# Side-by-side runs in the first layer, a_lo products one step behind, and x, weights and biases on other queues, in a four-layer graph network on one core

## The reference, cut to what matters

```python
h = jnp.maximum(_layernorm(x, axis=-1), 0.0)
x = x + L0(h)      # A_row @ h @ W_in + A_col @ h @ W_out, A and A.T each divided by its row sums
h = jnp.maximum(_layernorm(x, axis=-1), 0.0)
x = x + L1(h)      # two passes: swish(adj @ h @ W + b), then again on the result
h = jnp.maximum(_layernorm(x, axis=-1), 0.0)
x = x + L2(h)      # relu(D A_hat D @ h @ W + b), A_hat = adj + I, D from its row sums
h = jnp.maximum(_layernorm(x, axis=-1), 0.0)
x = x + L3(h)      # relu(D A_hat D @ (h @ W) + b)
```

## Time and profile before

| | before |
|---|---|
| median of three runs | 1110.06 us |
| the profiled execution, its own time | 1109.7 us |
| its span in the profile | 1107.9 us |
| TensorE matmuls busy | 1093.9 us (99%) |
| VectorE busy | 1044.1 us (94%) |
| ScalarE busy | 921.6 us (83%) |
| GpSimd busy | 31.4 us (3%) |
| mean rate from and to HBM | 368 GB/s |
| granted TensorE clock, mean | 1.00 of full speed |

### The profile page before, as it was taken

How to read it: one execution, slowest core, us unless ns; L and a number is a source line. 1 busy time by engine, 2 the same in 40 slices (tenths; PEclk the granted TensorE clock), 3 DMA queues, 4 the chain that set the end, 5 groups by cost and what they waited for, 6 DMA issues and landing times.

```text
span 1107.9 us, 14636 instructions
## 1 busy us (share of the span) xinstructions
PE 1093.9 (99%) x4992; PEld 909.1 (82%) x4992; DVE 1044.1 (94%) x1427; ACT 921.6 (83%) x1313; POOL 31.4 (3%) x30
## 2 busy tenths in 40 slices
PE   6999999999999999999999999999999999999998
PEld 5888888888888888888888888888888887888886
DVE  7899998999999999989989899999989999999997
ACT  7999997799788688888787788888888888887774
POOL 2000000000000000000000011121100000000000
PEclk9999999999999999999999999999999999999999
DMA  9999999999998999999999999999999999999992
GB/s 349 409 409 406 403 404 352 367 390 409 369 370 314 345 409 409 409 399 363 340 376 402 382 344 362 355 364 367 359 393 349 380 348 359 381 366 405 356 359 112
DMA packets 113835, 408.35 MB, mean 369 GB/s; under 512 B 12641, under 2 KB 13921, under 8 KB 113761
## 3 DMA queue, kind: packets, MB, share of 16 engines
q1 hardware_dynamic: 113760, 407.42, 96.6%
HBM read 405.27 MB, written 2.10 MB: 368 GB/s over the span
## 4 chain that ended last, share of the span: by engine, by line
PE 85%; DVE 13%; issue 1%; DMA 1%; ACT 0%; SPq 0%; ACTq 0%
PE bank L806 54%; PE bank L810 27%; DVE a_lo L553 10%; PE bank L827 3%; DVE stats L611 1%; DMA raw<-in_adj_t_dram 1%; DVE x_sb L705 0%; DVE zt L696 0%; DVE raw L547 0%; DVE h_lo L604 0%; PE bank L817 0%; DVE mv L615 0%; DVE acc L547 0%; PE bank L819 0%; DVE lnscale L627 0%
## 5 line engine op out<-in xcount | busy, mean ns | idle before, releaser
L553 DVE TENSOR_TENSOR a_lo<-raw,a_hi 128x1024 fp32r<-128x1024 f32 x560 | 657.5, 1219 | 31.1 <-ACT a_hi L410 14.0
L806 PE MATMUL bank<-a_hi,h_hi 128*128 128x512 f32 x1400 | 436.7, 393 | 8.8 <-ACT a_hi L412 8.8
L410 ACT ACTIVATE a_hi<-raw 128x1024 fp32r<-128x1024 f32 x368 | 378.7, 1056 | 68.4 <-PE bank L810 57.7
L810 PE MATMUL bank<-a_lo,h_hi 128*128 128x512 f32 x1400 | 433.1, 391 | 0.9 <-DVE a_lo L553 0.8
L806 PE MATMUL bank<-a_hi,h_lo 128*128 128x512 f32 x1400 | 432.1, 390 | 0.0
L810 PEld LDWEIGHTS bank<-a_lo,h_hi 128*128 128x128 f32 x1400 | 262.5, 188 | 58.9 <-DVE a_lo L553 4.6
L806 PEld LDWEIGHTS bank<-a_hi,h_hi 128*128 128x128 f32 x1400 | 260.3, 189 | 60.1 <-issue 8.7
L806 PEld LDWEIGHTS bank<-a_hi,h_lo 128*128 128x128 f32 x1400 | 263.6, 188 | 55.3
L412 ACT ACTIVATE a_hi<-raw 128x1024 fp32r<-128x1024 f32 x192 | 201.9, 1054 | 24.5 <-PE bank L810 10.6
L553 DVE TENSOR_TENSOR a_lo<-acc,a_hi 128x1024 fp32r<-128x1024 f32 x144 | 170.7, 1217 | 6.3 <-ACT a_hi L410 4.6
L410 ACT ACTIVATE a_hi<-acc 128x1024 fp32r<-128x1024 f32 x144 | 147.6, 1060 | 23.9 <-PE bank L810 22.6
(11 more groups left out here) (79 smaller groups left out, 403.3 us busy)
## 6 DMA issues: line engine op xcount, KB each, us to landing
raw<-in_adj_t_dram SPq DMA_DIRECT2D x496, 512.0 KB, 7.0
acc<-in_adj_t_dram SPq DMA_DIRECT2D x144, 512.0 KB, 6.3
raw<-in_adj_dram SPq DMA_DIRECT2D x128, 512.0 KB, 8.0
out_dram<-x_sb SPq DMA_DIRECT2D x7, 256.0 KB, 4.6
x_sb<-in_x_dram SPq DMA_DIRECT2D x3, 512.0 KB, 9.1
x_sb<-in_x_dram SPq DMA_DIRECT2D x2, 256.0 KB, 3.1
out_dram<-x_sb SPq DMA_DIRECT2D x2, 128.0 KB, 1.7
w_sb<-in_L_gnn_W_dram SPq DMA_DIRECT2D x3, 64.0 KB, 9.0
```

The lines of the kernel that those rows point to most:

```text
L410: act.activation(sub_hi_of(n), sub_raw(n), ACT.Copy).then_inc(sub_hi, 1)
L553: dve.tensor_tensor(sub_lo_of(n), sub_raw(n), sub_hi_of(n).bitcast(F32), ALU.subtract).then_inc(sub_lo, 1)
L806: pe.matmul(bank[half][:, :], weights, hi_a[:, half * GW:(half + 1) * GW], start=start and weights is hi_w, stop=False)
L810: last = pe.matmul(bank[half][:, :], hi_w, lo_a[:, half * GW:(half + 1) * GW], start=False, stop=stop)
```

## The change

It does five things.

- **Order.** The three first runs go side by side: block 0 with d = 1, 2, 3, then block 1, and so on, steps 0 to 23. That makes blocks 2 and 3 of h due at step 6, 4 and 5 at step 12, 6 and 7 at step 18. The next run (number 3) takes the fourth pair of banks, and all later ones move to another pair (`run_banks`, `run_prior`, `pair_of`).
- **a_lo behind.** From step 4 on TensorE does the a_lo pair of a step behind the a_hi matmuls of the next one (`LO_BEHIND`). ScalarE's place is free once the a_hi matmuls of its former step are done (`hi_used`) and VectorE has read it; VectorE now waits for `sub_used` itself, with each a_lo.
- **The first layer norm.** Blocks 0 and 1 stay with VectorE. Blocks 2 to 7 go the way of the later ones, in pairs: bias by VectorE, Relu and h_hi by ScalarE, h_lo by VectorE, at the steps in the tables. GpSimd does none.
- **Queues.** ScalarE asks for x blocks 0 and 1 at its start, 2 and 3 behind its step 0, 4 to 7 behind its step 3. GpSimd asks for the rest of x, the weights and the biases, each behind a step of VectorE. SyncE has tiles alone.
- **Drains.** The copies of the first three runs stand behind steps 25 to 30.

```diff
+        for i in range(CB):
+            for d in range(1, NG):
+                seq.append((d - 1, 0, d, i, i == 0, i == CB - 1))
+                if i == CB - 1:
+                    runs.append((0, d, 0))
+                    run_end.append(len(seq) - 1)
         for b in range(NG):
-            for kind in range(2):
+            for kind in range(1 if b == 0 else 0, 2):
...
+        def run_banks(r):
+            return z_ps if r == 3 else run_ps[r % 3 if r < 3 else (r - 1) % 3]
+
+        def run_prior(r):
+            return None if r <= 3 else r - 4 if r <= 6 else r - 3
...
-        DRAIN = {run_end[r] + 7 - 3 * (runs[r][2] >= 2) + half: (r, half) for r in range(len(runs)) for half in range(2)}
+        DRAIN = {run_end[r] + (4 + r if r < 3 else 7, 7, 4, 4)[runs[r][2]] + half: (r, half)
+                 for r in range(len(runs)) for half in range(2)}
...
-        FIRST_STATS = {24: 4, 36: 5, 50: 6, 64: 7, 77: 8, 90: 9}
+        FIRST_STATS = {2: 1, 6: 2, 11: 3, 24: 4, 36: 5, 50: 6, 64: 7, 77: 8, 90: 9}
-        FIRST_AFFINE = {29: 4, 41: 5, 55: 6, 69: 7, 82: 8, 95: 9}
-        FIRST_RELU = {32: 4, 44: 5, 58: 6, 71: 7, 84: 8, 97: 9}
+        FIRST_AFFINE = {3: 1, 8: 2, 13: 3, 29: 4, 41: 5, 55: 6, 69: 7, 82: 8, 95: 9}
+        FIRST_RELU = {4: 1, 9: 2, 14: 3, 32: 4, 44: 5, 58: 6, 71: 7, 84: 8, 97: 9}
...
-        LOAD_X = {16: 2, 36: 3, 62: 4}
-        LOAD_W = {72 + 3 * i: i for i in range(5)}
-        LOAD_B = {87 + 3 * i: i for i in range(3)}
+        X_BLOCKS = [FIRST[0], FIRST[1], (GB, CB)] + [(b, b + CB) for b in range(CB, NB, CB)]
+        LOAD_X_ACT = {0: 1, 3: 2}
+        LOAD_X = {8: 3, 28: 4, 54: 5}
+        LOAD_W = {62 + 3 * i: i for i in range(5)}
+        LOAD_B = {77 + 3 * i: i for i in range(3)}
...
@@ gpsimd
+            for n in range(S0):
+                if n in LOAD_X or n in LOAD_W or n in LOAD_B:
+                    pool.wait_ge(sub_lo, n + 1)
+                if n in LOAD_X:
+                    i = LOAD_X[n]
+                    blocks = slice(*X_BLOCKS[i])
+                    pool.dma_start(x_sb[:, blocks, :], x[:, blocks, :]).then_inc(x_in[i], 16)
...
@@ scalar
                 if sub_before[n] is not None:
-                    act.wait_ge(sub_used, sub_before[n] + 1)
+                    act.wait_ge(sub_lo, sub_before[n] + 1)
+                    act.wait_ge(hi_used, sub_before[n] + 1)
...
@@ vector
                 dve.wait_ge(sub_hi, n + 1)
+                if sub_before[n] is not None:
+                    dve.wait_ge(sub_used, sub_before[n] + 1)
...
@@ tensor
+            def products(n):
+                hi_products(n)
+                if n > LO_BEHIND:
+                    lo_products(n - 1)
+                if n < LO_BEHIND:
+                    lo_products(n)
```

More of the change, by code:

```diff
@@ L35, in build_gnn_stack @@
     S0 = 2 * NG * NB
+    LO_BEHIND = 3
     ctx = ExitStack()
@@ L82, in build_gnn_stack @@
         std0, rstd0, bias0 = (zt[:, 384 + i * NB:384 + (i + 1) * NB] for i in range(3))
-        x_in = [sem(f"x_in{i}") for i in range(NG + 1)]
+        x_in = [sem(f"x_in{i}") for i in range(NG + 2)]
         const_in = sem("const_in")
@@ L374, in _ @@
                                base=0, pattern=[[-1, P]], channel_multiplier=1).then_inc(ident_made, 1)
[L376 to L387, removed]
+            weights = (w_in, w_out, w1, w2, w3)
+            biases = (b1, b2, b3)
+            for n in range(S0):
[5 more added lines that the diff above has]
+                    pool.dma_start(x_sb[:, blocks, :], x[:, blocks, :]).then_inc(x_in[i], 16)
+                if n in LOAD_W:
+                    i = LOAD_W[n]
+                    pool.dma_start(w_sb[:, i, :], weights[i]).then_inc(const_in, 16)
+                if n in LOAD_B:
+                    i = LOAD_B[n]
+                    pool.dma_start(b_sb[:, i, :], biases[i].rearrange("(a n) -> a n", a=1).to_broadcast([P, D]))\
+                        .then_inc(const_in, 16)
             for q in range(NQ):
@@ L799, in _, with operands, hi_products @@
         def _(pe):
-            def products(n, hi_w, lo_w, bank, start, stop):
-                hi_a, lo_a = sub_hi_of(n), sub_lo_of(n)
+            def operands(n):
+                if n < S0:
+                    r, _, _, k, first, last = seq[n]
+                    return h_hi[0][:, k, :], h_lo[0][:, k, :], run_banks(r), first, last
+                sweep, g, k = passes[n - S0]
+                src = SET_OF[sweep - 1]
+                return h_hi[src][:, k, :], h_lo[src][:, k, :], banks_of(sweep, g), k == 0, k == NB - 1
+            def hi_products(n):
+                hi_w, lo_w, bank, start, _ = operands(n)
                 pe.wait_ge(sub_hi, n + 1)
@@ L805, in products, with lo_products @@
                     for half in range(2):
-                        pe.matmul(bank[half][:, :], weights, hi_a[:, half * GW:(half + 1) * GW],
-                                  start=start and weights is hi_w, stop=False)
+                        last = pe.matmul(bank[half][:, :], weights, sub_hi_of(n)[:, half * GW:(half + 1) * GW],
+                                         start=start and weights is hi_w, stop=False)
+                last.then_inc(hi_used, 1)
+            def lo_products(n):
+                hi_w, _, bank, _, stop = operands(n)
                 pe.wait_ge(sub_lo, n + 1)
                 for half in range(2):
-                    last = pe.matmul(bank[half][:, :], hi_w, lo_a[:, half * GW:(half + 1) * GW], start=False, stop=stop)
+                    last = pe.matmul(bank[half][:, :], hi_w, sub_lo_of(n)[:, half * GW:(half + 1) * GW],
+                                     start=False, stop=stop)
                 last.then_inc(sub_used, 1)
+            def products(n):
[4 more added lines that the diff above has]
+                    lo_products(n)
             def tail_products(n, hi_w, lo_w, bank, half, stop):
@@ L863, in _ @@
             for n in range(S0):
-                r, _, _, k, first, last = seq[n]
-                if first and r >= 3:
-                    copied, added = drained(r - 3)
+                r, _, _, k, first, _ = seq[n]
+                if first and run_prior(r) is not None:
+                    copied, added = drained(run_prior(r))
                     pe.wait_ge(part_copied, copied)
@@ L873, in _ @@
                             pe.wait_ge(h_ready, i + 1)
-                products(n, h_hi[0][:, k, :], h_lo[0][:, k, :], run_ps[r % 3], first, last)
+                products(n)
                 first_layer(n)
@@ L887, in _ @@
                     pe.wait_ge(h_ready, split_n(sweep - 1, k // GB) + 1)
-                products(n, h_hi[src][:, k, :], h_lo[src][:, k, :], banks_of(sweep, g), k == 0, k == NB - 1)
+                products(n)
                 first_layer(n)
```

118 lines of the change are left out of this document (40 added, 78 removed).

## The result

The changed kernel takes 1111.59 us (median of 22 runs, 1111.04 to 1112.26), the kernel before, measured beside it, 1110.12 (22 runs, 1109.64 to 1111.08). The ratio is 1.0013, with a 95% interval of 1.0007 to 1.0019: 1.5 us more, inside the 0.2% that counts as no change. The profiled execution took 1111.62 us and has a span of 1109.8, 1.9 longer than before.

A forecast was written before the change was run, and what follows sets the result against it. TensorE, busy 1093.9 of 1107.9 us, was taken as the bound. Profiled 1109.7 + 1.6 (beginning) - 1.42 (a_lo) = 1109.9, against the median 1110.2; case 1109.3 to 1111.3 (chance 0.52), 8-in-10 range 1107.4 to 1112.8.

The forecast's parts named there:

- signs of being wrong: Bank pairs waiting for a_hi at other places, VectorE waiting for x, a_lo spaced 1.2 apart, or step 33 before 57.
- a_lo one step later, gain 1.42: TensorE's seven a_lo stalls after step 33, 2.76 us together: 0.25, 0.26 and 0.91 go, 1.34 stays.
- The stall near 147: TensorE waiting before an a_lo pair; one of two short, isolated stalls (0.25, 0.26 us) that both go.
- The debt of VectorE: Last five stalls, 2.25 us, where VectorE has no idle time from 820.15 to 968.99: 0.91 go, 1.34 stay.
- The beginning, loss 1.15 at step 15: Chain of ScalarE Relus and VectorE biases: step 15 starts on TensorE at 33.1, where 31.96 was due.
- The first bias: VectorE's bias for blocks 2 and 3, behind a_lo of step 3: ready at 14.1.
- the second rival: x blocks 2 and 3 land at 15.0, 3.1 late, delaying biases, step 15 and end: 1113.3; chance 0.13.
- TensorE starts around 7: First matmuls start near 7 instead of 8.75, with 128 KB of x beside the first tile.
- Drains, loss 0.45: ScalarE's six copies of the side-by-side runs, behind steps 25 to 30, make step 33 another 0.45 us late.
- x and weights by GpSimd, 0: GpSimd's loads of x blocks 8 to 15 and weights cost 0, with 20 us of room for x.
- The first rival: All seven stalls go, 2.76 us gained, and the beginning loses only 0.4: 1107.7; chance 0.21.
- The third: Second semaphore on each a_lo breaks VectorE's overlap, 1.22 instead of 1.13 each: 1119 at least; chance 0.04.

The follow-up runs named there:

- experiment 3: Kernel before with only the a_lo pair one step behind, including the extra TensorE increment and second semaphore on each a_lo: 1108.92 us, ratio 0.9987.
- experiment 5: Changed kernel with x blocks 0 and 1 asked for by SyncE ahead of its tiles instead of by ScalarE beside them: 1110.55 us, ratio 1.0005.
- Experiment 2: Changed kernel with x blocks 2 and 3 asked for at ScalarE's start, and blocks 4 to 7 behind step 0: 1110.32 us, ratio 1.0003.
- Experiments 4: Kernel before with queues alone changed: ScalarE asks for x blocks 0 to 7 at its start, GpSimd for other x, weights and biases: 1111.44 us, ratio 1.0012.
- experiment 8: Kernel before with GpSimd asking for later x, weights and biases; the first 512 KB of x stay with SyncE ahead of tiles: 1110.27 us, ratio 1.0002.
- Experiment 1: Changed kernel with the small Relu of blocks 2 and 3, and its h_lo, one step later: table steps 5, 10, 15: 1109.06 us, ratio 0.9991.
- experiments 6: Changed kernel with small Relus at 5, 10, 15, large ones at 36 and 47 instead of 32 and 44, last bias sooner: 1109.46 us, ratio 0.9993.
- experiment 9: Changed kernel with small Relus at 5, 10, 15, large ones spread to 36, 51, 62, 73, 85, 97, last bias sooner: 1107.92 us, ratio 0.9981.
- experiment 10: Changed kernel with Relus at 5, 10, 15, 36, 51, 62, 73, 85, 97; x blocks 0-1 by SyncE first, 2-3 at ScalarE's start: 1107.75 us, ratio 0.9980.

## Why the prediction was right, and where not

The forecast was 1110.2 in a case of 1109.3 to 1111.3; it came out at 1111.59: no change, as predicted, but 0.3 us above that case's own range. Two of the prediction's own signs of being wrong were there: VectorE waits for x (1.24 us), and a bank pair waits for a_hi at a new place (148.57). The terms, in the order of the prediction:

- **a_lo one step later, gain 1.42.** From step 33 to the end the changed kernel gains 3.35 - 1.88 = 1.47. The sum is right and its parts are not, so that it came out is in part luck. The stall near 147 did not go; it became one of a_hi (0.34), which experiment 3 shows as the price of the new order at each Relu that waits. The debt of VectorE gave back 1.28 instead of 0.91. Of its five stalls the first three are gone and the fourth fell from 0.71 to 0.49, while the last stayed at 0.67: my "can be spent only once" is right for the last one. The rest is more than the 0.91 allowed, by 0.18 in the five stalls and by 0.19 in places I had not listed. Why was not tested.
- **The beginning, loss 1.15 at step 15.** This is the mis-sized term: 34.66 - 31.96 = 2.70. Its links were right: 8.00 and 8.33 between the Relus (8.06 and 8.37), 2.42 from the last Relu to TensorE (2.54), waits of 1.18 (about 1.4). The first bias was not: used at 15.91 where I had 14.1. 1.24 of it is VectorE's wait for x blocks 2 and 3, which the second rival named, deciding "from 6 us after its issue". Issued at 7.51 and not around 6, they were there at 13.7, 6.2 later; not 9.1. The later issue is not all of it: in experiment 5 they were asked for at 5.34 and landed 7.5 later, at 12.88. Experiment 2 takes exactly this away and gets 1.22 back at step 15. The rest is that blocks 0 and 1 were there at 5.53, so that the a_lo of steps 0 to 2 ran from 8.99.
- **TensorE starts around 7.** Wrong by 2.1 us, and the step that failed is that "128 KB of x go beside the first tile" and cost nothing. Experiments 4 and 5 show the cost of a load beside tiles from both sides. That the start itself matters little was right: 2.48 us sooner are 0.82 at step 15.
- **Drains, loss 0.45.** 0.48 measured, at the place named. Step 33 was expected "near 58"; with the 1.55 of the term before it is 59.6, measured 59.66.
- **x and weights by GpSimd, 0.** Right, by experiment 8. Three loads of 512 KB landed after 7.3 to 8.0 us, where SyncE's queue took 9.1, and nothing waited for them. The Trainium skill (SBUF — State Buffer, section SBUF: two separate sides) warns of late ones while VectorE is in a two-port mode; nothing of the kind shows here, and whether any of VectorE's work here is in such a mode no run tells.
- **Sum.** 1109.9 for the profiled execution, plus 1.55 for the first bias and 0.03 for the drains, less 0.05: 1111.4. It took 1111.62.

Of the rivals, the second was at work in part (1.24 of its 3.1). The Trainium skill's rule that DMA engines take turns between queues (DMA: Bandwidth & Descriptors, section Queues, rings and completion order) agrees with the trace as far as it goes: x is not behind all tiles. Blocks 2 and 3, asked for at 7.51, landed at 13.71, while the last four tiles asked for before them (4.02 to 6.19) landed at 14.88 to 19.41. But a turn is not free, and the prediction had priced the first load as if it were. The first rival, in which all seven stalls go and the beginning costs little, has nothing for it here. The third is refuted.

What neither the forecast nor a rival had is that the loss hung on one place in a table. I had computed that ScalarE would wait at its Relu and priced it as a given chain. Experiment 1 shows that with the Relu one a_hi further back the chain is not there: the wait falls away, and with it what the late x costs.

## What to carry to other kernels

When two engines in order hand work to each other in turn, a wait costs all that stands behind it in the waiting engine's row, and that includes the work from which the awaited value is made. Put the consumer one item further back and count the loop again; here it was worth 2.5 us, more than the change as a whole cost. A stall that is taken away at one place comes back at the next unless the engine's lead between the two pays for both; moving the pieces of an engine needs the sum over a stretch, as experiments 6 and 9 show with the same pieces.

## What was not expected of the hardware

- A small load is not small beside a stream. 128 KB asked for at 0.74 were used from 2.97 when they stood ahead of the tiles in their queue and from 5.31 to 5.53 when they were asked for at the same time by another one (experiment 1 and the changed kernel); 128 KB more on that other queue left it at 5.34. It is the tile that costs, and not the other queue: in experiment 10, where 128 KB stood at 0.74 on each of the two queues and the first tile behind them, they landed at 3.47 and 3.64.
- TensorE's first matmuls take 1.05 to 1.06 us a pair, later ones 0.62 (starts 0.85 and 0.46 apart). The profile's windows give the granted clock as 1.00 in both stretches, but the trace's record of it begins only where the fast pairs do, at 12.42 in the changed kernel and at 14.98 in experiment 1. So no row has the clock of the slow stretch; by its pace, near half, it is the lower of the two levels (1.2 and 2.4 GHz), which is inferred and not shown. With nearly the same start, and without a pause of TensorE in it, the slow stretch lasted until about 15 us in two kernels (starts 8.88 and 8.94, experiments 1 and 6) and until about 12.5 in two others (9.10 and 9.00, the changed kernel and experiment 9); why was not tested. Some 1.2 us hang on it at step 3, and next to nothing at step 15.
